# Storing the query halves once and building a head's 64 rows in another order

## The reference

```
x = x + 0.5 * ffn(layernorm(x))
x = x + attention(layernorm(x))
x = x + 0.5 * ffn(layernorm(x))
# attention, 16 heads of size 16:
q = einsum('bsd,hde->bhse', x, wq) + bq          # k and v likewise
scores = softmax(einsum('bhse,bhte->bhst', q, k) / 4)
att = einsum('bhst,bhte->bhse', scores, v)       # then heads side by side, @ wo.T + bo
# ffn: three products with +-1 weights, relu between them, hidden size 1024
```

## Time and profile before

| | |
|---|---|
| time, median of 3 runs | 1477.49 us |
| profiled execution: its own time | 1477.21 us |
| profiled execution: span of the core | 1472.8 us |
| PE busy | 1464.3 us, 99% |
| ACT busy | 1149.7 us, 78% |
| DVE busy | 600.6 us, 41% |
| granted TensorE clock | 1.000 |
| DMA engines, mean busy share of the main queue | 24.1% |

### The profile page before, as it was taken

The page is one execution under the profiler, slowest core; times in us unless marked ns, Lnnn a source line. Parts: engine busy times, 40 slices in busy tenths (PEclk is TensorE's granted clock), DMA queues, the critical chain, the costliest instruction groups (busy, mean ns, idle before and its releaser), DMA issues.

```text
span 1472.8 us, 69969 instructions
## 1 busy us (share of the span) xinstructions
PE 1464.3 (99%) x32431; PEld 757.0 (51%) x32431; DVE 600.6 (41%) x1330; ACT 1149.7 (78%) x1240; POOL 60.1 (4%) x65
## 2 busy tenths in 40 slices
PE   8999999999999999999999999999999999999999
PEld 4555455544467447545454454455555455445454
DVE  7546745612431353335332343342351342333461
ACT  3221221799999999999999999999999999999821
POOL 2010111001000100010100000000000000000000
PEclk9999999999999999999999999999999999999999
DMA  5131324312231331223212312212212212212110
GB/s 140 47 86 36 90 76 108 92 47 81 73 75 43 99 90 58 75 86 97 92 47 72 94 47 71 89 51 68 83 54 71 75 54 71 75 58 67 26 36 17
DMA packets 113943, 103.66 MB, mean 70 GB/s; under 512 B 59638, under 2 KB 99318, under 8 KB 113646
## 3 DMA queue, kind: packets, MB, share of 16 engines
q1 hardware_dynamic: 112686, 98.20, 24.1%
q10 hardware_dynamic: 960, 0.92, 0.3%
HBM read 61.34 MB, written 25.15 MB: 59 GB/s over the span
## 4 chain that ended last, share of the span: by engine, by line
PE 98%; DVE 1%; DMA 1%; issue 0%; ACTq 0%; ACT 0%
PE psum L908 31%; PE psum L949 30%; PE psum L929 15%; PE psum L802 12%; PE psum L814 3%; PE psum L790 3%; PE psum L821 2%; PE psum L834 1%; DVE den_t L1177 0%; DMA den_t<-o_sb 0%; DMA den_t<-den_rows 0%; PE psum L827 0%; DMA x_sb<-in_x 0%; DVE att_t L1179 0%; ACTq L1343 0%
## 5 line engine op out<-in xcount | busy, mean ns | idle before, releaser
L1006 ACT ACTIVATE prob<-psum 128x1024 f32<-128x1024 f32 x1024 | 1031.8, 1026 | 57.0 <-PE psum L929 18.2
L949 PE MATMUL psum<-prob,v_sb 64*17 64x512 f32 x8192 | 546.4, 589 | 0.0
L929 PE MATMUL psum<-q_st,k_st 64*32 64x512 f16 (+1 forms) x7736 | 448.9, 376 | 0.3 <-issue 0.3
L979 ACT ACTIVATE h_hi<-psum 128x512 f16<-128x512 f32 x183 | 108.3, 597 | 210.4 <-PE psum L802 156.6
L929 PEld LDWEIGHTS psum<-q_st,k_st 64*32 64x32 f16 (+1 forms) x7736 | 146.3, 93 | 200.2 <-ACT prob L1006 91.6
L949 PEld LDWEIGHTS psum<-prob,v_sb 64*17 64x17 f32 x8192 | 149.5, 93 | 144.8 <-issue 90.9
L1046 DVE SCALAR_TENSOR_TENSOR h_lo<-psum,h_hi 128x512 f16<-128x512 f32 x256 | 168.3, 687 | 82.8 <-ACT h_hi L979 80.3
L1044 DVE TENSOR_SCALAR h_hi<-psum 128x512 f16<-128x512 f32 x73 | 50.5, 692 | 352.3 <-PE psum L908 352.3
L908 PE MATMUL psum<-h_lo,w 64*32 64x512 f16 (+1 forms) x4688 | 161.6, 376 | 0.8 <-issue 0.7
L908 PE MATMUL psum<-h_hi,w 64*32 64x512 f16 (+1 forms) x4688 | 160.2, 376 | 0.3 <-ACT h_hi L979 0.2
L908 PEld LDWEIGHTS psum<-h_hi,w 64*32 64x32 f16 (+1 forms) x4688 | 84.7, 93 | 60.5 <-issue 14.5
(11 more groups left out here) (110 smaller groups left out, 882.5 us busy)
## 6 DMA issues: line engine op xcount, KB each, us to landing
k_st<-k_halves SPq DMA_DIRECT2D x256, 128.0 KB, 2.8
q_halves<-piece SPq DMA_DIRECT2D x32, 256.0 KB, 2.5
q_st<-q_halves SPq DMA_DIRECT2D x64, 128.0 KB, 2.6
x_rows<-x_sb SPq DMA_DIRECT2D x16, 256.0 KB, 2.2
k_halves<-piece SPq DMA_DIRECT2D x16, 256.0 KB, 2.9
x_sb<-x_rows SPq DMA_DIRECT2D x32, 128.0 KB, 2.5
out_y<-x_sb SPq DMA_DIRECT2D x16, 256.0 KB, 2.3
att_rows<-o_sb SPq DMA_DIRECT2D x120, 32.0 KB
```

Of the source, the lines that this page charges most:

```text
L929: mm = pe.matmul(psum[c, SCORES[(h + r) % len(SCORES)], :], k_st[rows, slot, t * P:(t + 1) * P][:, c], q_st[rows, slot, :], start=True, st ...
L949: mm = pe.matmul(psum[32 * j:32 * j + va, O_BANKS[r], :], v_sb[rows, b * key_tiles + t, GROUP * g4 + j, :], prob[rows, h % PROBS, :], star ...
L979: act.activation(hi, psum[:, bank, :], ACT.Relu).then_inc(act_done, 1)
L1006: act.activation(prob[:, to:to + 2, :], psum[:, bank:bank + 2, :], ACT.Exp, scale=score_scale / QK_SCALE ** 2).then_inc(exp_sem, 1)
```

## The change

Queries are stored once: `q_dram` loses its duplicated axis, and the 32 query stores of 256 KB become 16. The order of a head's 64 rows changes. Before, the partition inside a slot was (feature, half of k, copy) for keys and (feature, copy, half of q) for queries, over the 32 features of two heads. Now a head has its own 64 partitions: for keys (half of k, feature, copy), for queries (copy, feature, half of q). A key load still fills 32 partitions with 128 KB from 16 DRAM rows of 4 KB, each for two neighbouring partitions, but takes the rows of one half. The query load of a pair becomes two loads, one per head, of 64 partitions each; the source pattern is 2 (repeated) x 32 x 512, the repetition being its outermost axis. A group so has 12 loads in place of 10, in the same ten turns. `STAGE` and `pieces_out` count accordingly.

```
-        q_dram = internal("q_halves", (dim, 2, 2, tokens), F16)
+        q_dram = internal("q_halves", (dim, 2, tokens), F16)
-        STAGE = 16 * 2 * (KEY_PARTS + 1)
+        STAGE = 16 * 2 * (KEY_PARTS + 2)
         def pieces_out(m, n):
-            return 16 * n * (2 - m % 2)
+            return 16 * n
                 elif s.kind == "qk":
-                    if m % 2:
-                        sp.dma_start(k_dram[dims, :, columns], piece[:, m]).then_inc(piece_out[m], 16)
-                    else:
-                        for half in range(2):
-                            sp.dma_start(q_dram[dims, half, :, columns], piece[:, m]).then_inc(piece_out[m], 16)
+                    sp.dma_start((q_dram, k_dram)[m % 2][dims, :, columns], piece[:, m]).then_inc(piece_out[m], 16)
             if part < KEY_PARTS:
-                rows = 4 * hd // KEY_PARTS
-                k_rows = k_dram[dims, :, keys].rearrange("d c t -> (d c) t")[part * rows:(part + 1) * rows, :]
-                sp.dma_start(k_st[2 * rows * part:2 * rows * (part + 1), slot, :],
-                             k_rows.unsqueeze(1).broadcast_to((rows, 2, seq))).then_inc(staged[g % 2], 16)
+                head, term = divmod(part, 2)
+                rows = slice((h + head) * hd, (h + head + 1) * hd)
+                sp.dma_start(k_st[2 * hd * part:2 * hd * (part + 1), slot, :],
+                             k_dram[rows, term, keys].unsqueeze(1).broadcast_to((hd, 2, seq))).then_inc(staged[g % 2], 16)
             else:
-                sp.dma_start(q_st[:, slot, :], q_dram[dims, :, :, queries].rearrange("d k c t -> (d k c) t")
-                             ).then_inc(staged[g % 2], 16)
+                for head in range(2):
+                    rows = slice((h + head) * hd, (h + head + 1) * hd)
+                    q_rows = q_dram[rows, :, queries].rearrange("d c t -> (d c) t")
+                    sp.dma_start(q_st[4 * hd * head:4 * hd * (head + 1), slot, :],
+                                 q_rows.unsqueeze(0).broadcast_to((2, 2 * hd, BANK))).then_inc(staged[g % 2], 16)
```

## The result

The changed kernel takes 1479.37 us (median of 22 runs, 1477.49 to 1481.12) against 1477.32 us (22 runs, 1476.31 to 1478.24) for the kernel before: a ratio of 1.0016, 95% interval 1.0010 to 1.0022. By the medians it is 2.05 us slower, inside the 3 us (0.2%) that the prediction called no change, and outside chance. The profiled execution took 1478.76 us, its span is 1474.6.

What follows compares the result with a forecast made beforehand. PE was taken to bound the kernel, idle for 8.5 of 1472.8 us; 0 from stores, keys and queries, plus 4.4 us outside the span, kept 1477.2 us profiled and 1477.5 us median, range 1475.5 to 1480.0 us.

Steps and rivals of the forecast that it cites:

- 0 from the queries: Query loads in attention: 64 of 128 KB become 128 of 64 KB, landing within their leads; 0 us on the span.
- the tight place: Shortest lead of a group's last query load, 541.29 to 551.53: 7.7 us needed of 10.24, so PE waits for none.
- a couple of single waits of 1 us: Allowance in the main case's range of 1475.5 to 1480.0 us, beside 0.6 us in the tight place.
- The stores: Query stores, 32 become 16: 4.19 MB less on the main queue, 4.8 us less of SP, 0 on the span.
- The keys: Key loads, rows at double distance in DRAM: at most +2.3 us of latency, taken as 0; 0 on the span.
- Issue on SP: Query loads on SP: 0.552 us each, 70.7 us in all, +47.9; neither that nor +22.8 reaches PE by itself.
- Two engines, 3.2 us of moving for a pair: A pair's query loads queue on two engines: 3.2 us moving in place of 0.4, second landing 5.4 us after first issue.
- The rule of the Trainium skill: For query loads: a leading zero-stride broadcast of c copies confines the DMA to at most c engines; 5.4 us landing.
- Leads: Last query load of a group to the next turn of groups: mostly 10.8 to 11.5 us, 6.0 needed; PE waits for none.
- No transfer sets the pace today: Whole kernel: PE's longest wait is 1.6 us and none names a DMA, so cheaper transfers have nothing to shorten.
- DVE held up: Rival: transposes, x rows and fetches land 1 to 3 us late, PE waits for DVE's low halves; 11 us, chance 0.03.

Runs made afterwards that it cites:

- copies apart: The changed kernel with each of the two copies of a head's query rows loaded by its own DMA, four per pair: 1475.95 us against 1476.78, ratio 0.9994.
- by half: Kernel before with queries stored once and a pair's queries in two 64 KB loads, one per half, outermost axis 32: 1476.31 us against 1476.78, ratio 0.9997.
- on two: Kernel before plus two idle 64 KB DMAs behind each query load, outermost axis 2: 1489.54 us against 1476.78, ratio 1.0084.
- on sixteen: Kernel before plus two idle 64 KB DMAs behind each query load, from 64 partitions, outermost axis 64: 1476.83 us, ratio 0.9999.
- wide: Kernel before with matmuls of 128 columns in place of four of 32: 1593.70 us against 1477.42; with two further two-engine DMAs behind each query load, 1593.71.

## Why the prediction was right, and which term was not

- **The forecast**, no change within 0.2% and 1475.5 to 1480.0 us, held: 1479.37. The time of 1477.5 is 1.9 us too low, and the sum's last step, "0 from the queries", is the one that failed: they cost 2.05 us. That the range still held it is in part luck. Its upper part was there for an unknown price in the tight place and for "a couple of single waits of 1 us", and the loss turned out to be a few stops of that size, but of a kind that the prediction did not consider.
- **The stores: 0.** 4.2 MB less on the main queue, as worked out (98.20 to 94.00), and no gain before attention.
- **The keys: 0.** Shown by the run with the copies apart (0.9994).
- **Issue on SP:** 0.552 us was taken from the denominator fetch, 0.525 measured. More issues than that cost nothing in two experiments.
- **Two engines, 3.2 us of moving for a pair:** 3.2 us measured. The rule of the Trainium skill that was weighed (DMA: Bandwidth & Descriptors, Rules for kernel authors) holds here for c = 2 too.
- **Leads.** No wait of PE names the query or key loads. The tightest, from a pair's first query issue to the next group's release, became 9.84 us (540.54 to 550.38).
- **What was missed.** "No transfer sets the pace today" was read from waits that name a DMA. The transfers that PE depends on most closely have no semaphore: its own instructions, 257 packets of 16 KB, one every 4.5 us in the median in attention. Late ones show as "issue". The rule about few engines was priced only by what the confined transfer itself has to meet, not by what shares its two engines. With the two-engine loads some of these packets take longer and more of them come late, some while a transpose is under way; a few times per execution PE runs dry for 1 us. The rival that ended slower (DVE held up, 11 us) had part of the right place, transposes and fetches that share the two engines, but the wrong way to PE: DVE's wait for denominators rose only from 12.2 to 13.6 us.

What is shown: the outermost axis of 2 is what costs (copies apart, by half, on two against on sixteen); the time goes at the places where a piece of PE's program ends (27 gaps of 27); and the cost needs PE's high rate of instructions (wide). What is argued is the last link, that a piece of program waits behind data or a held-up transpose on the same engine; no view here names the engine of a packet, and in four of the 27 gaps PE went on only 3.1 us and more after the last packet had ended.

## What to carry to other kernels

Read a repeated row with the repetition as an inner axis, or as a DMA of its own, so that the outermost axis is long: 32 and 64 places cost nothing here, 2 and 4 did where 128 such loads were issued. Cutting one transfer in two cost nothing, confining it did. In a kernel that issues many small matmuls, ask of every transfer not only whether it lands in time but what it does to the program fetches; look for "issue" waits on weight loads that stand between two instructions of one tile, and count whether they lie a whole number of program pieces apart. Compare two traces by a marker that repeats, since PE's busy time hides gaps of 1 us.

## What the runs showed of the hardware

- The gaps of over 0.9 us in PE's weight loads stand at the same instruction of every 256, where one 16 KB packet of its program ends; in 23 of 27 PE went on 1.3 to 1.6 us after the end of a packet.
- A long gap can cost again. In the run with more on two engines, behind the gap of 2.64 us in PE's matmuls that ended at 1123.26, the granted clock fell from 1.00 to 0.50, that is to 1.2 GHz, for some 3 us (columns as in the earlier trace rows):

```profile
1120.00:1123.20 3.20, 0.62 (x24) 0.12 (x8) 0.00 (x0) 1.66 (x2) 0.00 (x0) 1.00 0.29 66
1123.20:1124.40 1.20, 1.14 (x48) 0.66 (x56) 0.05 (x1) 0.00 (x0) 0.00 (x0) 0.97 0.06 14
1124.40:1126.00 1.60, 1.60 (x24) 0.34 (x16) 1.57 (x3) 1.51 (x2) 0.00 (x0) 0.50 0.00 0
1126.00:1128.00 2.00, 2.00 (x40) 0.74 (x29) 0.37 (x1) 1.03 (x1) 0.00 (x0) 0.56 0.20 66
```

- A DMA transpose behind two short transfers on two engines took 9.6 us to land and held SP for 6.3 us, against 4.6 and 2.0.
- Four matmuls of 32 columns in place of one of 128 are worth 116 us of 1594 in this kernel. In the wide form PE's weight loads at the scores wait 365 us for "issue":

```profile
L929 PEld LDWEIGHTS psum<-q_st,k_st 64*128 64x128 f16 x2048 | 98.9, 93 | 482.3 <-issue 365.2
```
